# A graph network on one core: ten edge tiles per layer fetched row by row from SP instead of five, and two padding tiles left out

## The reference

```
h = relu(layernorm(x)); x = x + L0(h): segment_sum((h @ W)[src], dst) / count + b
h = relu(layernorm(x)); x = x + L1(h): lap = segment_sum(h[src] * edge_weight, dst); leaky((h+lap)@W1 + (h*lap)@W2 + b), normed
h = relu(layernorm(x)); x = x + L2(h): segment_sum((h @ Wn)[src] * net(edge_attr), dst), then a two-product MLP
h = relu(layernorm(x)); x = x + L3(h): graph attention with 4 heads: softmax over the edges of a dst, then W3, layernorm, relu
```

## Time and profile before

| what | value |
|---|---|
| median of 3 runs (range) | 4280.39 us (4277.88 to 4283.37) |
| the profiled execution | 4279.49 us, its span 4278.2 us |
| busy: POOL, DVE, PE, ACT | 71%, 61%, 57%, 43% |
| gathers by POOL | 3116 of 944 ns |
| TensorE clock granted, mean | 0.775 |

### The profile page before, as it was taken

How to read it: one execution, slowest core, us unless ns; L and a number is a source line. 1 busy time by engine, 2 the same in 40 slices (tenths; PEclk the granted TensorE clock), 3 DMA queues, 4 the chain that set the end, 5 groups by cost and what they waited for, 6 DMA issues and landing times. The chain is left out here.

```text
span 4278.2 us, 67483 instructions
## 1 busy us (share of the span) xinstructions
PE 2426.0 (57%) x13354; PEld 1993.2 (47%) x13354; DVE 2590.9 (61%) x7217; ACT 1825.3 (43%) x4203; POOL 3046.2 (71%) x3220
## 2 busy tenths in 40 slices
PE   2665666654565656566444444444566666666667
PEld 1454544444444444456344443443445455455556
DVE  4444454443566666668444344443348999999998
ACT  3444444421244444432211111111257887878875
POOL 3777777776777777777477777777646777777764
PEclk8788787866677777778666666656678999999999
DMA  4444444432344343432233333333238222222221
GB/s 130 117 114 123 123 121 117 123 84 63 92 118 119 113 121 110 120 103 71 68 107 108 103 107 108 108 107 108 81 82 142 57 57 57 57 57 57 57 50 31
DMA packets 233932, 405.81 MB, mean 95 GB/s; under 512 B 61850, under 2 KB 132463, under 8 KB 233520
## 3 DMA queue, kind: packets, MB, share of 16 engines
q0 software_dynamic: 99968, 207.33, 19.8%
q10 hardware_dynamic: 65776, 121.56, 10.1%
q1 hardware_dynamic: 67784, 72.61, 5.5%
HBM read 332.15 MB, written 67.78 MB: 93 GB/s over the span
## 5 line engine op out<-in xcount | busy, mean ns | idle before, releaser
L675 POOL DMA_INDIRECT t_work<-d_T,t_tabG x3116 | 2942.9, 944 | 1080.8 <-issue 918.2
L1175 DVE TENSOR_TENSOR t_acc<-t_acc,ps 128x128 f32 (+1 forms) x732 | 210.5, 288 | 763.1 <-PE ps L559 470.3
L1118 PE MATMUL ps<-t_work,t_acc 128*128 x2592 | 419.3, 323 | 250.8 <-SPq L734 223.3
L1118 PEld LDWEIGHTS ps<-t_work,t_acc 128*128 128x128 f32 x2592 | 389.9, 234 | 314.5 <-issue 314.0
L559 PE MATMUL ps<-t_acc,t_wts 128*128 128x512 f32 x392 | 312.4, 943 | 336.7 <-DVE t_acc L598 336.7
L1164 DVE TENSOR_TENSOR t_acc<-t_work,ps 128x512 f32<-128x512 f32 x244 | 167.2, 685 | 553.3 <-ACT ps L1243 552.9
L1243 ACT COPY ps<-t_acc 128x512 f32 x244 | 140.4, 588 | 841.1 <-SPq L734 834.9
L1118 PE MATMUL ps<-t_acc 128*128 128x128 f32 x1296 | 283.1, 407 | 370.1 <-DVE t_acc L1164 370.0
L1118 PEld LDWEIGHTS ps<-t_acc 128*128 128x128 f32 x1296 | 262.0, 309 | 390.9 <-DVE t_acc L1164 390.9
L1648 PE MATMUL ps<-t_work,t_hT 128*128 x1960 | 318.4, 311 | 98.5 <-DVE t_acc L1658 84.3
L1648 PEld LDWEIGHTS ps<-t_work,t_hT 128*128 128x128 f32 x1960 | 268.1, 212 | 159.5 <-issue 159.5
(11 more groups left out here) (190 smaller groups left out, 4656.4 us busy)
## 6 DMA issues: line engine op xcount, KB each, us to landing
d_edge_net<-t_acc ACTq DMA_DIRECT2D x98, 512.0 KB
t_acc<-d_edge_net SPq DMA_DIRECT2D x98, 512.0 KB
t_work<-d_T,t_tabG POOLq DMA_INDIRECT x3116
t_acc<-in_edge_attrT ACTq DMA_DIRECT2D x96, 512.0 KB, 4.1
t_acc<-d_T SPq DMA_DIRECT2D x1280, 0.5 KB
t_acc<-d_T SPq DMA_DIRECT2D x640, 0.5 KB
t_work<-d_T SPq DMA_DIRECT2D x640, 0.5 KB
t_acc<-d_T ACTq DMA_DIRECT2D x12, 790.1 KB, 17.4
```

The source lines that it names most:

```text
L675: pool.indirect_dma_start(out=work[:, at:at + width], out_offset=None, in_=table, in_offset=bass.IndirectOffsetOnAxis(ap=idx[:, g * QUAD + ...
L1118: last = pe.matmul(sums(layer, s, width), masks[s % MASKS][:, k, :], rows_k, start=(k == 0), stop=(k == QUAD - 1))
L1175: dve.tensor_tensor(out=o, in0=o, in1=sums(layer, s, width), op=ALU.add).then_inc(e_acc[layer], 1)
```

## The change

SP fetches ten tiles a layer (groups 29, 47, 65, 84, 102, 120, 138, 157, 175, 193), seven rows in each of the first 183 steps. The indices come as 20 rows of 64 numbers from a new input `sides` in HBM to two small buffers on partition 0, and one load takes up to seven of them to registers. The two tiles of the last group that hold no edge are not gathered. POOL issues 772 gathers a layer. Nothing that the output holds is changed.

```diff
-SIDE, SIDE_PER = 5, 4
+SIDE, SIDE_PER, SIDE_READ = 10, 7, 64
+SIDE_READS = SIDE * P // SIDE_READ
...
+        def gathers_of(g):
+            return min(QUAD, ET - QUAD * g) - (g in SIDE_AT)
...
-                for k in range(QUAD - (g in SIDE_AT)):
+                for k in range(gathers_of(g)):
...
+        def side_sources(layer, c):
+            row = acc[0:1, NT * ACC3:XC] if layer < 3 else work[0:1, (RING * QUAD + 2) * ROW3:]
+            return row[:, c % 2 * SIDE_READ:(c % 2 + 1) * SIDE_READ].bitcast(I32)
...
+        def read_sources(layer, c):
+            sp.dma_start(side_sources(layer, c), a["sides"][0:1, c * SIDE_READ:(c + 1) * SIDE_READ])\
+                .then_inc(s_src[c % 2], 16)
...
-            for j in range(SIDE):
-                at = QUAD * SIDE_AT[j] + QUAD - 1
-                for p in range(max(SIDE_PER * (n - SIDE_BEGIN[j]), 0), min(SIDE_PER * (n + 1 - SIDE_BEGIN[j]), P)):
-                    row, = numbers(ENG.SP, idx[p:p + 1, at:at + 1], 1, 0, N - 1)
+            for c in range(SIDE_READS):
+                lo, hi = [min(max(SIDE_PER * m - SIDE_READ * c, 0), SIDE_READ) for m in (n, n + 1)]
+                if lo == hi:
+                    continue
+                if lo == 0:
+                    sp.wait_ge(s_src[c % 2], 16 * (SIDE_READS // 2 * layer + c // 2 + 1))
+                found = numbers(ENG.SP, side_sources(layer, c)[:, lo:hi], hi - lo, 0, N - 1)
+                for r, row in zip(range(c * SIDE_READ + lo, c * SIDE_READ + hi), found):
+                    j, p = divmod(r, P)
                     sp.dma_start(side_rows(layer, j)[p:p + 1, 0:width], table[bass.ds(row, 1), :])\
                         .then_inc(s_row[layer][j % 4], 16)
+                if hi == SIDE_READ and c + 2 < SIDE_READS:
+                    read_sources(layer, c + 2)
...
-            return sum(16 * (QUAD - (m in SIDE_AT)) for m in range(n % RING, n + 1, RING))
+            return sum(16 * gathers_of(m) for m in range(n % RING, n + 1, RING))
...
+            for c in range(2):
+                read_sources(layer, c)
             ahead = AHEAD if layer < 3 else AHEAD + 2
```

More of the change, by code:

```diff
@@ L40 @@
 assert STEPS % 2 == 0
+SIDE_READS = SIDE * P // SIDE_READ
+assert P % SIDE_READ == 0
 assert SIDE_AT[-1] < GROUPS
@@ L686, in build @@
         s_row = [[sem(f"s_row{layer}{k}") for k in range(4)] for layer in range(4)]
+        s_src = [sem(f"s_src{k}") for k in range(2)]
         def side_rows(layer, j):
@@ L691, in side_rows @@
             return (acc if layer < 3 else work[:, RING * QUAD * ROW3:])[:, lo + j % 2 * width:lo + (j % 2 + 1) * width]
-        assert MLP + 11 * GRP + 2 * ACC3 <= BB * ACC3 and (RING * QUAD + 2) * ROW3 <= work.shape[1]
+        def side_sources(layer, c):
+            row = acc[0:1, NT * ACC3:XC] if layer < 3 else work[0:1, (RING * QUAD + 2) * ROW3:]
+            return row[:, c % 2 * SIDE_READ:(c % 2 + 1) * SIDE_READ].bitcast(I32)
+        assert MLP + 11 * GRP + 2 * ACC3 <= BB * ACC3 and NT * ACC3 + 2 * SIDE_READ <= XC
+        assert (RING * QUAD + 2) * ROW3 + 2 * SIDE_READ <= work.shape[1] and SIDE_READS % 2 == 0
+        def read_sources(layer, c):
+            sp.dma_start(side_sources(layer, c), a["sides"][0:1, c * SIDE_READ:(c + 1) * SIDE_READ])\
+                .then_inc(s_src[c % 2], 16)
         def fetch_rows(layer, table, n):
             width = table.shape[1]
-            for j in range(SIDE):
-                at = QUAD * SIDE_AT[j] + QUAD - 1
-                for p in range(max(SIDE_PER * (n - SIDE_BEGIN[j]), 0), min(SIDE_PER * (n + 1 - SIDE_BEGIN[j]), P)):
-                    row, = numbers(ENG.SP, idx[p:p + 1, at:at + 1], 1, 0, N - 1)
+            for c in range(SIDE_READS):
[7 more added lines that the diff above has]
+                    j, p = divmod(r, P)
                     sp.dma_start(side_rows(layer, j)[p:p + 1, 0:width], table[bass.ds(row, 1), :])\
                         .then_inc(s_row[layer][j % 4], 16)
+                if hi == SIDE_READ and c + 2 < SIDE_READS:
+                    read_sources(layer, c + 2)
         def place_rows(layer, table, pitch, j):
@@ L1851 @@
         "lastg": lastg.reshape(2, P).T, "lastrow": lastg[:GROUPS].reshape(1, GROUPS),
+        "sides": np.concatenate([src[QUAD * g + QUAD - 1] for g in SIDE_AT]).reshape(1, SIDE * P),
         "idx": src[:TILES].T, "dsts": dst[:TILES].T, "wgt": weight[:TILES].T,
```

## The result

The changed kernel takes 4357.15 us (median of 4 runs, 4347.4 to 4363.97), the kernel before, in the same comparison, 4281.6 us (4 runs, 4277.88 to 4283.37). The ratio is 1.0176 with a 95% interval of 1.0158 to 1.0194: slower by about 76 us, where 24 us less were predicted, and outside the range of 4249 to 4265. The profiled execution took 4355.7 us, its span is 4354.4 us, 76.2 longer than before.

A forecast was written before the change was run, and what follows sets the result against it. POOL's gather issue was taken to bound layers 0, 2 and 3, not layer 1. Terms -8.7 + 1.3 - 8.7 - 7.5 = -23.6 us gave 4256.5 us; own range 4252 to 4262, 8-in-10 range 4249 to 4265.

The forecast's parts named there:

- SP's work added: SP's relay step: seven rows at 0.47, load 0.60, other 0.3, together 4.2 us against POOL's 4.92 a group; costs nothing.
- SP becomes the pacer: Rival: runs of seven row DMAs on SP issue too slowly, step 5.8 us, some 4900 us in all; chance 0.06.
- SP's waits for landings gone in layer 0: Sign of being wrong: SP no longer waits for landings in layers 0 and 3; before, 238.7 us in layer 0.
- 7r + 0.9 = 4.92: Point where SP's step overtakes POOL's pace, r being the time of a row; reached at 0.57 us a row.
- some 4900 us: Kernel time if SP paces: a 5.8 us step, 161 us over POOL's pace in each layer.
- layer 3 as the one to feel it first: If SP's slack and the ring's cover went, late groups would first hit DVE in layer 3, with 34.3 us of room.
- Seven gathers fewer, where POOL sets the pace: Each layer loses seven POOL gathers of 1.248 us; all counts in layers 0 and 2, -8.7 us each.
- Layer 3, -7.5 us: Seven gathers fewer, but DVE's last wait gives back only 1.33 us of the padding's 2.5; bounds 8.7 and 5.0.
- Layer 1, +1.3 us: PE and node rows set the end; a later landing near group 171 and later row fetching lengthen it; bounds -3.7 and +4.
- POOL's last hold: Layer 1: POOL is held by a full ring the last time at 1890.23, group 163, then has 5 us a group.
- the bound of +4: Upper bound for layer 1's loss, in us: a whole relay step.
- The rival that transfers pace: Rival: transfers, not POOL's issuing, pace; only padding counts, 2 us, kernel stays at 4278; chance 0.07 with other no-change ways.

The follow-up runs named there:

- pad8_d: Changed kernel with indices stored eight to a step (seven used, one filler), loaded from a multiple of eight words; 4263.05 us, 16 us less than the kernel before.
- per8_d: Changed kernel with eight rows a step instead of seven and the buffer at a multiple of eight words; 4249.88 us, 27.5 us faster than the kernel before.
- rows4: Kernel before, still five side tiles and four rows a step, with one aligned load of four indices and padding not gathered; 4267.34 us against 4277.92, ratio 0.9976.

## Why the prediction was wrong

**The step that failed** is the price of the index load in "SP's work added": "no load of seven on SP is in the trace, the nearest are 0.509 us for one value on SP and 0.597 us for eight on DVE. I take 0.60." It is 1.48 us. Both ends of that bound were right for what they measured and neither bounds this load. One number costs 0.28 to 0.51 us, eight at a multiple of four words 0.69, seven 1.1 there and 1.5 to 1.8 elsewhere. The price is not monotonic in the count, and it depends on the first word, which a step of seven never keeps. A bound "between one and eight" was taken for a bound on seven.

The total of that sum came out with the aligned load, by luck in its parts. The prediction made a step 4.2 us of SP's work; pad8_d has 4.22. A row is 0.41 us and not 0.47 (seven DMAs and their addresses in one piece), the semaphores and the relay's other load 0.7 and not 0.3, by 4.22 - 7 x 0.41 - 0.69 (0.5 with the mean of the loads, 0.83, for their median). These two differences cancel. A small slip beside them: a chunk border adds a second load in 17 of 183 steps, not in one of nine.

**Which rival it was.** "SP becomes the pacer", held at 0.06, is what happened: SP's waits for landings gone in layer 0, PE's waits for SP up, SP's queue first in the chain. Its place was wrong. It was put on the row issues, which stayed at 218 to 225 ns, and its decision point, 7r + 0.9 = 4.92, has the load as the fixed 0.6 in that 0.9. Written with the load l as the unknown, 7 x 0.41 + l + 0.7 = 4.92, it decides at l = 1.35 us. The size was wrong with the place: "some 4900 us" was for 0.9 us a step over POOL's pace, it is 0.3. 183 steps of 0.30 us (layer 0) and 0.27 us (layer 2) are 55 and 50 us, and against pad8_d the layers lost +33.6, +17.7, +40.9 and +2.2 us. What is missing, 21 us in layer 0 and 9 in layer 2, I put down to the ring's eight groups and the 13 steps without rows at the end; that is argued, not measured. The prediction named layer 3 as the one to feel it first. It felt it least: its step of 4.98 holds 32.7 us of waits over 174 steps (28.8 for landings, the rest for PE), so SP's own work is 4.80 us there, just under POOL's. A good half of the 0.37 us to layer 0's 5.17 are its loads, 1.52 us a step by the single loads against 1.73; the rest is open.

**Seven gathers fewer, where POOL sets the pace.** Right, once the load is out of the way. First to last gather is as forecast in all four layers of pad8_d. Layer 0 gives -9.8 and -10.1 us for -8.7. Layer 2 gives -11.1 in per8_d: -8.7 up to the last gather, exactly, and 2.4 behind it, where the stretches up to layer 3's first gather differ in the clock that was granted. By windows, first the kernel before, then per8_d (length; busy us of PE, PEld, DVE, ACT, POOL; granted clock):

```profile
3071.00:3173.00 102.00, 79.36 (x390) 52.58 (x390) 46.87 (x189) 68.38 (x163) 31.86 (x34) 0.79 0.19 49
```

```profile
3050.00:3150.00 100.00, 74.40 (x390) 49.85 (x390) 49.01 (x192) 68.71 (x164) 31.92 (x35) 0.86 0.19 50
```

The same 390 matmuls took 5 us less at 0.86 than at 0.79. It is one execution of each, so I count the 2.4 us as no gain of the change. pad8_d's -13.3 parts in the same way: -8.7 up to the last gather and -4.6 behind it, in a stretch with a granted clock of 0.89:

```profile
3061.40:3159.20 97.80, 73.35 (x390) 48.56 (x390) 48.29 (x191) 68.76 (x164) 31.92 (x34) 0.89 0.19 51
```

**Layer 3, -7.5 us.** -4.7 and -6.6 us: just outside and inside the bounds of 5.0 and 8.7. From first to last gather both kernels gain 9 us, but the stretch behind the last gather grows from 121.5 us to 125.9 and 124.1. DVE's last wait for rows ended 4.2 us behind the last gather's start before; in pad8_d it ends 8.5 us ahead of it, at 4124.93, and in per8_d 9.5 us ahead:

```profile
4114.59 0.29 DVE L1589 TENSOR_TENSOR t_hT<-t_work,ps 128x128 f32<-128x128 f32 x1 [1.25 <-SPq L763]
```

So DVE sets the end of this layer once the gathers are that early. It has less room than the single last wait of the earlier trace rows suggested.

**Layer 1, +1.3 us.** The sign was right and the size was not. The forecast said that the end hangs on the landings after POOL's last hold, and that rows to fetch after step 160 delay them. With rows until step 182 (pad8_d) the layer is 9.5 us longer, outside the bound of +4; with none after 159 (per8_d) it is 2.7 us shorter. The two kernels differ in one thing more: with eight rows a step all ten side tiles lie in groups 26 to 170, with seven the last two lie in groups 175 and 193, so POOL has two gathers more to issue up to group 171. At 1.25 us each these are 2.5 of the 12 us at most. PE's last long wait ends 4.7 us later in pad8_d than before, near the bound; the last pair begins 8.8 us later. The further 4.1 us do not lie in a wait for a landing, of which PE has none after 1929.63. They lie in its waits for ACT on the node rows, from 1929.7 to 2056.57 us:

```profile
PE ps L1038 <- ACT t_acc L1028: 22.8, 5, 8.9
```

Before it was 18.1 us, the longest 4.2. Why that one wait grew to 8.9 us, in this one execution, stays open.

**Issue or transfer.** The rival that transfers pace is refuted by pad8_d and per8_d: the same 5,120 row DMAs and the same bytes, and 16 and 27 us faster than before. The Trainium skill (DMA: Bandwidth & Descriptors, section Issuing engines are not separate DMA queues) says that another issuer saves only sequencer time, usually small beside the transfer. The first half fits these runs, the second does not: moving five more tiles a layer to SP is the larger part of per8_d's 27 us, while rows4, which moves none, gains 10.6. And the warning has a point here that I did not take from it: sequencer time was what the change spent, on SP.

**Left open.** Why three chips ran SP's queue at 0.7 us an instruction in stretches, and what held the other engines there. Alignment alone was run as a kernel of its own only on those three; on the others it is shown by the single loads of the changed kernel (1098 against 1632 ns), and in the kernel's time together with the removal of the second load at a chunk border (17 of 200 loads a layer). Leaving out the padding alone was run only on those chips as well, and gave 0 and -0.2% (4.4 and 10.6 us between the medians, 6.3 expected).

## What to carry to other kernels

A batched load to registers on SP has a price by its count and its first word, and a load of another size does not bound it: batches of four or eight from a multiple of four words, with filler where the work is in sevens, cost 0.47 and 0.69 us behind a row DMA, seven from elsewhere 1.47 to 1.83. When work is moved to an engine that relays for others, write its step as a sum with every term as an unknown in turn, and ask at which value it overtakes the pace; a term that has no row of its own, in a step with 0.7 us of slack, is the one to measure first. And look at what is fetched last: in layer 1, the kernel that fetched rows until 13 groups before the end was 12 us slower than the one that stopped 36 before it, though its side tiles also lay later.

## What the runs showed that was not expected

One word of offset made a load of eight numbers 1829 instead of 686 ns. Three numbers (828 ns) cost more than four aligned ones (470), both behind a row DMA, and a load right behind a DMA issue costs 0.16 us more than one right behind another load. In three of the seven comparisons, those at 5425, 5425 and 5503 us, the chip ran SP's instructions in stretches at 0.7 us each, in every kernel profiled there, and the order of the kernels turned round: per8 is 5% slower than before there and 0.6% faster where SP runs freely.
